# An LSTM over 512 steps on one core: where the turned gates and tanh c are kept, and where the loops begin

## The reference, cut to what matters

```python
xW = jnp.einsum('ntd,dk->tnk', x, Wx) + b          # x: 4 sequences, 512 steps, 256 features
c0 = jnp.zeros_like(h0)                            # h0 = cond, 4 x 256
def step(carry, xw_t):
    prev_h, prev_c = carry
    a = xw_t + prev_h @ Wh                         # Wh: 256 x 1024
    i = sigmoid(a[:, 0:256]);  f = sigmoid(a[:, 256:512])
    o = sigmoid(a[:, 512:768]); g = tanh(a[:, 768:1024])
    next_c = f * prev_c + i * g
    next_h = o * tanh(next_c)
    return (next_h, next_c), next_h
out = x + transpose(hs)                            # float32 throughout
```

## Time and profile before

| | us |
|---|---|
| median of 3 runs | 1056.75 |
| lowest and highest | 1054.12, 1073.64 |
| the profiled execution, its own time | 1052.39 |
| its span in the trace | 1050.3 |
| PE busy, share of the span | 1029.1, 98% |
| DVE busy | 697.8, 66% |
| ACT busy | 620.2, 59% |

### The profile page before, as it was taken

How to read it: one execution, slowest core, us unless ns; L and a number is a source line. 1 busy time by engine, 2 the same in 40 slices (tenths; PEclk the granted TensorE clock), 3 DMA queues, 4 the chain that set the end, 5 groups by cost and what they waited for, 6 DMA issues and landing times.

```text
span 1050.3 us, 105684 instructions
## 1 busy us (share of the span) xinstructions
PE 1029.1 (98%) x45316; PEld 835.7 (80%) x45316; DVE 697.8 (66%) x4453; ACT 620.2 (59%) x4610; POOL 0.7 (0%) x6
## 2 busy tenths in 40 slices
PE   5999999999999999999999999999999999999997
PEld 4888887888888887888888878888888878888885
DVE  4566666666666666666666666666666666666664
ACT  2466666556666666566666665566666665666664
POOL 0000000000000000000000000000000000000000
PEclk9999999999999999999999999999999999999999
DMA  3000000000000000000000000000000000000000
GB/s 91 5 7 7 6 6 7 6 6 7 6 6 6 6 6 6 6 7 6 6 7 6 6 7 6 6 7 6 6 7 6 6 7 6 6 7 6 6 6 7
DMA packets 32111, 8.76 MB, mean 8 GB/s; under 512 B 31584, under 2 KB 31584, under 8 KB 32096
## 3 DMA queue, kind: packets, MB, share of 16 engines
q1 hardware_dynamic: 31488, 8.41, 3.7%
q10 hardware_dynamic: 608, 0.14, 0.1%
HBM read 6.43 MB, written 2.10 MB: 8 GB/s over the span
## 4 chain that ended last, share of the span: by engine, by line
PE 98%; SPq 1%; issue 0%; DMA 0%; DVE 0%; ACT 0%; DVEq 0%
PE gates L414 28%; PE o_units L431 27%; PE x_acc L406 19%; PE f_units L423 12%; PE x_acc L372 7%; PE gates L380 2%; PE o_units L394 2%; PE f_units L387 1%; SPq L151 1%; DMA wh_raw<-in_L_cond_Wh_dram 0%; SPq L155 0%; DVE wh L237 0%; ACT scan_both L222 0%; DVE wh L234 0%; DVE a_bank L325 0%
## 5 line engine op out<-in xcount | busy, mean ns | idle before, releaser
L414 PEld LDWEIGHTS gates<-wh,h_pad 128*32 128x32 f32 x16384 | 333.1, 111 | 172.2 <-DVE h_pad L343 157.5
L414 PE MATMUL gates<-wh,h_pad 128*32 128x64 f32 x16384 | 425.6, 227 | 1.3 <-DVE h_pad L290 0.9
L216 ACT ACTIVATE tanh_f<-f_units 128x4 f32<-128x4 f32 x1024 | 175.1, 171 | 369.3 <-PE f_units L423 369.3
L423 PE MATMUL f_units<-h_pad,wh 128*32 128x4 f32 x16384 | 368.3, 173 | 0.7 <-issue 0.7
L423 PEld LDWEIGHTS f_units<-h_pad,wh 128*32 128x32 f32 x16384 | 329.1, 111 | 0.7 <-issue 0.7
L431 PE MATMUL o_units<-h_pad,wh_o 128*64 128x4 f32 x8192 | 327.1, 202 | 0.7 <-issue 0.7
L431 PEld LDWEIGHTS o_units<-h_pad,wh_o 128*64 128x64 f32 x8192 | 283.9, 139 | 8.7 <-issue 0.7
L325 DVE STREAM_TRANSPOSE a_bank<-gates 128x64 f32<-128x64 f32 x512 | 136.0, 266 | 163.8 <-PE gates L414 153.1
L406 PE MATMUL x_acc<-wh,zeros 128*32 128x256 f32 x772 | 240.3, 393 | 0.0
L336 DVE TENSOR_TENSOR_SCAN cell<-scan_both 128x12 f32<-128x12 f32 x1024 | 187.0, 183 | 68.0
L225 ACT ACTIVATE tanh_o<-o_units 128x4 f32<-128x4 f32 x1024 | 169.6, 166 | 12.8 <-PE o_units L431 4.5
(11 more groups left out here) (42 smaller groups left out, 258.3 us busy)
## 6 DMA issues: line engine op xcount, KB each, us to landing
x_next<-in_x_dram SPq DMA_DIRECT2D x256, 8.0 KB
x_here<-in_x_dram SPq DMA_DIRECT2D x256, 8.0 KB
out_dram<-y_rows SPq DMA_DIRECT2D x256, 8.0 KB
wx_raw<-in_L_cond_Wx_dram SPq DMA_DIRECT2D x8, 128.0 KB, 3.5
wh_raw<-in_L_cond_Wh_dram SPq DMA_DIRECT2D x8, 128.0 KB, 2.9
bias_raw<-in_L_cond_b_dram ACTq DMA_DIRECT2D x4, 32.0 KB, 3.1
h_rows<-in_cond_dram ACTq DMA_DIRECT2D x4, 1.0 KB
```

Source lines behind the costliest of these rows:

```text
L216: nc.scalar.activation(tanh_f[:, m, :], f_units[m][:, t * N:(t + 1) * N], ACT.Tanh).then_inc(tanh_f_done[m], 1)
L414: last = nc.tensor.matmul(gates[k][q * R:(q + 1) * R, columns], h_stationary(b, t), wh[:, b, q, k * W + columns.start:k * W + columns.stop ...
L423: last = nc.tensor.matmul(bank[q * R:(q + 1) * R, t * N:(t + 1) * N], wh[:, b, q, at:at + R], h_at(b, t - 1), start=False, stop=b == M - 1 ...
```

## The change

- `turned[k]` becomes columns 64 to 127 of the bank in which the gates k are summed, for both k; `tanh_c[m]` becomes four columns of the bank `o_units[m]`. `a_bank` and the two SBUF buffers go.
- PE's and DVE's loops begin at t = 3 (`LAP_END` is 2): t = 0 to 2 of the first chunk are written out, the body is t = 3 to 7 of chunk k and t = 0 to 2 of chunk k + 1, and t = 3 to 7 of the last chunk are written out. ACT's loop is as it was.
- No `keep_busy` in t = 2, before the jump back (and in the last chunk's t = 2), and none in t = 7 after the injects.
- The injects of a half wait for the tanh that reads its turned gates (`tanh_ig_done[m]`), since those now lie in the bank that the inject writes. They were behind one wait on both turns and both tanh of F.
- DVE turns the next x in t = 4, where it did in t = 2.

```diff
+    X_TURN_AT = 4
+    LAP_END = 2
...
-        a_bank = ps("a_bank", [128, 512])
-        turned = {BA: a_bank[:, 0:W], BB: sb("turned_b", [128, W])[:]}
-        tanh_c = [a_bank[:, W:W + N], sb("tanh_c1", [128, N])[:]]
+        turned = {k: gates[k][:, W:2 * W] for k in ROWS}
+        tanh_c = [o_units[m][:, W:W + N] for m in range(M)]
...
-                if ahead and t == 2:
+                if ahead and t == X_TURN_AT:
                     dve.wait_ge(x_next_loaded, (chunk + 2) * (Q * DMA))
                     nc.vector.transpose(x_units[:], x_next[:]).then_inc(x_turned, 1)
...
-            for t in range(STEPS):
+            for t in range(LAP_END + 1):
                 step(0, t, True, True)
-            with dve.Fori(1, CHUNKS - 1) as k:
-                for t in range(STEPS):
+            with dve.Fori(0, CHUNKS - 1) as k:
+                for t in range(LAP_END + 1, STEPS):
                     step(k, t, False, True)
-            for t in range(STEPS):
+                for t in range(LAP_END + 1):
+                    step(k + 1, t, False, False)
+            for t in range(LAP_END + 1, STEPS):
                 step(CHUNKS - 1, t, False, False)
...
-                elif t < STEPS - 1 or not ahead:
-                    keep_busy()
-                if ahead and t == STEPS - 1:
-                    for k in ROWS:
-                        pe.wait_ge(gates_turned[k], now)
-                    for m in range(M):
-                        pe.wait_ge(tanh_f_done[m], now)
-                    pe.wait_ge(x_part_turned, chunk + 2)
-                    inject_early()
+                elif ahead and t == STEPS - 1:
+                    for m in range(M):
+                        pe.wait_ge(tanh_ig_done[m], now)
+                        inject(AB[m])
+                        inject_units(f_units[m], BF, m)
+                elif t != LAP_END:
                     keep_busy()
...
+            for t in range(LAP_END + 1):
+                step(0, t, True)
             with pe.Fori(0, CHUNKS - 1) as k:
-                for t in range(STEPS):
+                for t in range(LAP_END + 1, STEPS):
                     step(k, t, True)
-            for t in range(STEPS):
+                for t in range(LAP_END + 1):
+                    step(k + 1, t, True)
+            for t in range(LAP_END + 1, STEPS):
                 step(CHUNKS - 1, t, False)
```

## The result

| | us |
|---|---|
| after, median of 4 runs (lowest to highest) | 1625.97 (1625.93 to 1626.06) |
| before, median of the 4 runs beside it | 1059.45 (1054.12 to 1073.64) |
| ratio, 95% interval | 1.537 (1.530 to 1.545) |
| profiled execution of after: own time, span | 1625.95, 1624.2 |

The changed kernel is 1.54 times as long. The forecast was 1030.

The account below looks back on a forecast made before the run. Latency on a loop through PE, DVE and ACT was taken as the bound. Savings of 0.27 + 0.14 less 0.015 make 0.395 us a chunk over 62 borders: 1027.3 on the profile's time, median 1030, range 1014 to 1061.

Parts of the forecast that it names:

- The calls on zeros held TensorE's clock: Rival on PE: removing two of six calls a chunk delays or loses full clock; chances 0.11 late, 0.11 lost.
- a clock that never rises: Extreme of the clock rival: 504 steps at the lower level would give 1675 us; no separate chance given.
- one or two chunks late: Clock rises one or two chunks later, 10.1 us each: 1040 to 1050 (1038 to 1055 in the odds), chance 0.11.
- the lost clock: Clock at the lower level for five chunks or more: slower, 1080 us and more, chance 0.11.
- The sum at full speed: All terms together: 0.395 us saved a chunk, giving 1027.3 us on the profiled execution's own time.
- The border: Step from t = 7 to t = 0: without jumps and call, 0.27 us saved a chunk (bounds 0.20 and 0.31).
- tanh c in PSUM: tanh c of m = 1 in PSUM: 0.020 us saved in seven of eight steps, 0.14 a chunk.
- The turn within one bank: DVE's turn(BA) reading and writing one bank: taken as 0, upper bound 0.06 us a step.
- The rival of 0.06 a step: One bank slower to turn in: 0.06 us in 512 steps costs 30.7, giving 1061; chance at full price 0.08.
- The jump between t = 2 and t = 3: PE's and DVE's moved jumps, thinly covered: 0.015 us lost a chunk (bounds 0 and 0.10).
- The turn of x: DVE turns x in t = 4, not t = 2: an extra 0.03 us moves with it, net 0.
- The wait of the injects for tanh: At the border, injects wait for the tanh of their turned gates instead of the turns: counted at nothing.

Follow-up runs that it names:

- e2: Kernel after the change with only the call on zeros of t = 2 put back; 1667.95 us, ratio 1.580.
- e11: Kernel after the change with a call on zeros of 64 columns behind the injects of t = 7; 1638.04 us, ratio 1.547.
- e1: Kernel after the change with only the call on zeros (256 columns) behind the injects of t = 7 put back; 1054.99 us, ratio 0.992.
- e9: Kernel after the change with the call on zeros of t = 3 replaced by 32 calls, eight per column group, in every chunk; 1211.0 us, one run.
- e10: Kernel after the change with a call on zeros of 128 columns behind the injects of t = 7; median 1057.8 us (1032.49 to 1081.37).
- e3: Kernel before with only the new places of turned gates and tanh c and the injects' new waits, all calls and loops kept; 1047.16 us, ratio 0.987.
- e12: Kernel after with a 192-column call behind the injects of t = 7 and 32 calls on zeros behind the first x products; 1037.56 us, ratio 0.973.
- e4: Kernel after the change with 32 products of zeros by 256 columns behind the first x products; 1623.25 us, ratio 1.538.
- e5: Kernel after the change with the call on zeros of t = 7 put back ahead of the injects instead of behind; 1046.52 us, ratio 0.998.
- e6: Kernel after, PE's loop split: 16 passes with the call behind the injects of t = 7, then 47 without; 1487.95 us, ratio 1.415.
- e7: Kernel before with 32 products of zeros behind the first x products and nothing else; 1049.92 us, ratio 0.996.
- e8: Kernel after with the call behind the injects of t = 7 and 32 products of zeros behind the first x products; 1044.86 us, ratio 0.989.

## Why the prediction was wrong

**The step that failed** is in the rival "The calls on zeros held TensorE's clock": "Against it: the x products and the injects stay, PE's pauses grow only by the 0.4 us of a missing call". The x products and the injects are not enough (after, e2, e11), and the size of PE's pauses was the wrong thing to weigh: what counted was one call of 256 columns at one place of the chunk, the one behind the injects, which is enough to bring the clock up (1054.99 in e1; 1667.95 in e2, with the call of t = 2 instead). Why that place does it stays open. The rival had the right mechanism, named the right call (the rise follows the one at 41.77) and got 0.11. Its price for a clock that never rises, 1675, was close to e2 (1668); after came out at 1626, because at the low level a missing call shortens the step (42 us, e2).

The profile before held the evidence to weigh it higher. Before's runs were 19.5 us apart, read in the prediction as "a matter of luck already". If the rise is by luck at one place of each chunk, then taking away what stands there may not delay it by a chunk or two but remove it. The cases in between, "one or two chunks late", had as much chance as the lost clock and did not happen: 64 columns never let it rise, 128 did so at the fifth border in one trace.

**The sum at full speed was nearly right.** Put together from e9 (the border) and e10 (the other steps), the kernel after the change at full speed would have a chunk of 1937 + 2000 + 1916 + 1895 + 1896 + 1897 + 1958 + 1908 = 15407 ns, against 15870: 0.46 less, where the forecast had 0.395. That would be 1052.4 - 62 x 0.463 = 1023.7 on the profile's own time, forecast 1027.3. By terms:

- *The border*, forecast 0.27: 2256 to 1937 is 0.32, but 0.06 of it is the new banks and the injects' new waits (e3, which does not split them), so 0.255 for call and jumps together. The stress lay wrong: moving the jumps alone gives nothing (e1 against e3), while the call off the border gives 0.258 when no jump stands there (e1 against e9). What a jump would cost at a border without a call was not tried; the 0.11 by which PE's first gates are later in e3 than in e1 says that it may not be nothing.
- *tanh c in PSUM*, forecast 0.020 a step: 0.025 (1921 to 1896). If tanh c is the cause, as forecast, PE took in most of its 33 ns; e3 moves the turned gates as well and does not split the two. At t = 0, where the border was thought to lose nothing by it, e3 gave 64. `hidden` takes 158 ns from the bank for both halves (e1), where it took 164 from SBUF. The Trainium skill's "VectorE: DVE Perf Modes", in its section on the TRN2 errata, has PSUM as the dearer source; the plain steps of e3, 25 ns shorter, don't bear that out.
- *The turn within one bank*, forecast 0: 265 ns against 266. The rival of 0.06 a step did not happen.
- *The jump between t = 2 and t = 3*, forecast 0.015: the step into t = 3 is 1895 in e1, like its neighbours. Nothing.
- *The turn of x*, forecast a move that gives nothing: right in the net, wrong in the size. The step into t = 2 falls by 12 (1925 in e3, 1913 in e1), not by 30, those into t = 4 and 5 do not grow, and the one into t = 7 grows by 10, for which I have no cause.
- *The wait of the injects for tanh*, forecast 0: the two groups of injects of e9 start at 598.70 and 598.89, and the gates at 599.22 follow the first half of h by 0.21 to 0.22, as in its plain steps. Right.

**The rule on the clock.** "TensorE: Matmul & The Clock Gate" of the Trainium skill says, in Part 1, that the throttled state is the default and activity releases it. The traces agree on the first: each starts at 1.2 GHz. As to the second, to be busy in the sense of the profile is not enough: its page counts PE busy for 99% of the span of after, and the clock never rose.

## What to carry to other kernels

A call that computes nothing may be what brings the matrix engine to full speed: before one is removed, look at where in the trace the clock rose (by the durations of the passes, not by the clock's line, which may show nothing) and what ran just ahead of it. Shorten such a call before dropping it: half of it, 128 columns, cost 38 ns at the border in place of 258 and still let the clock rise, though late in the run that was traced; a quarter, 64, did not. And a scatter from run to run of the size of a few slow passes of the loop is a hint that the rise is by chance at one place; an edit at that place should be given the price of never rising.

## What the runs showed of the hardware

- The clock can stay at 1.2 GHz for a whole execution of 1668 us with PE 99% busy by the page, and the trace then has no record of the clock: its page lacks the line and views by window read 1.00.
- Outside the added stretches of calls it rose only behind a border with a call, eleven times in nine traces, the lasting rises between 39 and 145 us. Each chunk that it comes late costs some 10 us (25.9 against 15.7 in e1), which accounts for the scatter of e12's runs; for the other kernels that is likely and was not worked out.
- PE stalls for 0.4 to 1.5 us on its first pass through new code, and most falls came up to 3.1 us after such a stall: in e4 (30.49, then 32.6), e5 (47.39, 49.4), e6 (47.73, 49.5; 296.48, 298.6), e7 (30.12, 32.3), e8 (22.59, 23.5), e9 (43.38, 44.2) and e12 (22.50, 25.6). The last chunk, written out, does the same in e5 and e7 (1031.92, then 1032.4; 1025.12, then 1025.6). But a stall need not bring a fall: none came within 8 us of those of 0.95 at 22.76 in e7 and of 0.97 at 1037.96 in e3. That the stall is the cause was not tested.
- A product on one column group holds up only that group. But turn(BA) waits for all four, so one group that was late cost the whole step 0.26 at the border.
